# Feed-forward weights loaded, rounded and checked inside the first cross-attention

## The reference, cut to what matters

```python
x = x + tanh(g_xattn[0]) * L0_xattn(layernorm(x), ctx, ctx)      # 16 heads of 16
x = x + tanh(g_ffn[0])   * L0_ffn(layernorm(x))
x = x + tanh(g_xattn[1]) * L1_xattn(layernorm(x), ctx)           # 8 heads of 64
x = x + tanh(g_ffn[1])   * L1_ffn(layernorm(x))                  # gated self-attention
...
# L0_ffn: tlin(x, w, s) = (x @ w.T) * s
h = silu(tlin(x, w1, w1_s)) * tlin(x, w2, w2_s)    # w1, w2: 1024 x 256
h = gelu(tlin(h, h1, h1_s))                        # h1, h2: 1024 x 1024
h = gelu(tlin(h, h2, h2_s))
out = tlin(h, w3, w3_s)                            # w3: 256 x 1024
```

## Time and profile before

| | |
|---|---|
| Time, median of 3 runs | 2078.14 us (2077.79 to 2080.9) |
| Profiled execution, its own time | 2080.15 us |
| Its span in the trace | 2078.3 us |
| Mean granted TensorE clock | 0.956 |
| Busy over the span | PE 1858.6, DVE 1202.1, ACT 1129.6, POOL 736.7 us |

### The profile page before, as it was taken

How to read it: one execution, slowest core, us unless ns; L and a number is a source line. 1 busy time by engine, 2 the same in 40 slices (tenths; PEclk the granted TensorE clock), 3 DMA queues, 4 the chain that set the end, 5 groups by cost and what they waited for, 6 DMA issues and landing times. The chain is left out here.

```text
span 2078.3 us, 61778 instructions
## 1 busy us (share of the span) xinstructions
PE 1858.6 (89%) x27201; PEld 1516.5 (73%) x27201; DVE 1202.1 (58%) x1661; ACT 1129.6 (54%) x1952; POOL 736.7 (35%) x832
## 2 busy tenths in 40 slices
PE   4999509999999999999599986899999999999986
PEld 3677407888878888888477865778888878887865
DVE  4776463423233243332455444888888888887883
ACT  3777444434344344443255542667777777776661
POOL 3777460000100010001233321456655565654541
PEclk9999859999999999999799996999999999999997
DMA  3010240000000000000301003422332242223210
GB/s 88 27 33 23 107 165 1 21 1 21 13 9 20 0 20 20 0 20 0 116 17 38 23 21 102 110 63 64 89 105 59 59 120 79 65 69 99 59 49 23
DMA packets 135939, 104.92 MB, mean 50 GB/s; under 512 B 9379, under 2 KB 132104, under 8 KB 135688
## 3 DMA queue, kind: packets, MB, share of 16 engines
q1 hardware_dynamic: 135688, 101.19, 16.0%
HBM read 76.00 MB, written 25.17 MB: 49 GB/s over the span
## 5 line engine op out<-in xcount | busy, mean ns | idle before, releaser
L1487 ACT ACTIVATE E_prob<-E_ps_s,E_negmax 128x1024 f32<-128x1024 f32 x256 | 284.7, 1115 | 146.9 <-DVE E_negmax L1801 146.5
L1801 DVE TENSOR_REDUCE E_negmax<-E_ps_s 128x1 f32<-128x1024 f32 x256 | 301.4, 1219 | 92.6 <-PE E_ps_s L1306 92.4
L1808 DVE STREAM_TRANSPOSE E_prob<-E_prob 128x1024 f32<-128x1024 f32 x256 | 303.9, 1226 | 23.8 <-ACT E_prob L1487 11.5
L1325 PEld LDWEIGHTS E_ps_o<-E_prob,E_vrep 32*64 32x64 f32 x15872 | 232.1, 130 | 71.5 <-ACT E_part L1513 54.5
L1325 PE MATMUL E_ps_o<-E_prob,E_vrep 32*64 32x128 f32 x15872 | 264.8, 274 | 18.6 <-issue 9.3
L909 ACT ACTIVATE F_raw<-F_ps,ffn_scales 128x512 f32<-128x512 f32 x128 | 88.2, 689 | 288.2 <-PE F_ps L819 288.2
L819 PE MATMUL F_ps<-F_ha,ffn_w_rounded 128*128 128x512 f32 x1024 | 240.5, 396 | 0.0
L819 PE MATMUL F_ps<-F_hb,ffn_w_rounded 128*128 128x512 f32 x1024 | 240.2, 395 | 0.0
L819 PEld LDWEIGHTS F_ps<-F_hb,ffn_w_rounded 128*128 128x128 f32 x1024 | 192.4, 188 | 46.5
L819 PEld LDWEIGHTS F_ps<-F_ha,ffn_w_rounded 128*128 128x128 f32 x1024 | 191.3, 188 | 47.9 <-issue 1.6
L1703 POOL TENSOR_TENSOR E_part<-E_part 128x512 f32<-128x512 f32 x93 | 119.3, 1283 | 255.1 <-ACT E_part L1513 255.1
(11 more groups left out here) (275 smaller groups left out, 3984.6 us busy)
## 6 DMA issues: line engine op xcount, KB each, us to landing
E_vrep<-E_v_all SPq DMA_DIRECT2D x128, 256.0 KB, 3.0
W_stage<-in_L_ffn_h_wT SPq DMA_DIRECT2D x16, 512.0 KB, 6.1
E_v_all<-E_vst SPq DMA_DIRECT2D x32, 256.0 KB, 2.2
F_x<-x SPq DMA_DIRECT2D x9, 512.0 KB, 3.7
A_x<-in_x SPq DMA_DIRECT2D x16, 256.0 KB, 5.4
x<-A_x SPq DMA_DIRECT2D x16, 256.0 KB, 2.2
x<-F_x SPq DMA_DIRECT2D x8, 512.0 KB, 2.9
C_x<-x SPq DMA_DIRECT2D x16, 256.0 KB, 5.4
```

The source lines that it names most:

```text
L1325: mm = pe.matmul(low[64 * j:64 * j + 64, g, :], vrep[rows, slot, KB // 4 * (quarter % 2) + k, dh * j:dh * (j + 1)], prob[rows, u % 2, :, j ...
L1487: act.activation(prob[:, s // UT % 2, s % UT, j, :], ps_s[:, j, :], ACT.Exp, bias=negmax[:, at:at + 1], scale=1.0, accum_out=den[:, 2 * c ...
L1801: dve.tensor_reduce(negmax[:, at:at + 1], ps_s[:, j, :], AX.X, ALU.max, negate=True).then_inc(d_max, 1)
L1808: dve.transpose(at, at).then_inc(d_t, 1)
```

## The change

The block W goes. `cross_attention` takes a further argument `ffn`, given for A alone. In A, SP loads the 22 chunks into a stage of 3 places. At the end of each step T = -4 to 17 ACT rounds one chunk by the same copy as before. DVE no longer takes differences: it ors the 32 bits of the staged chunk into `w_bits` (the first time an and with 0x7FFFFF), at the end of the same step. At the end of T = 18 it masks the 23 mantissa bits of the result and takes the maximum per partition: the flag is zero only if all weights have an empty mantissa. TensorE transposes this column ahead of `scores(28)`, at T = 26, into columns of `ps_s` that no score uses, and DVE takes its maximum into `ffn_inexact`. POOL has no part in it. The flag is then read as before. A place in the stage must be free of both ACT and DVE before a chunk is loaded over it. The buffer of the rounded weights is reserved throughout A.

```diff
+WCH = 1024
+STAGE = 3
+CHECK_FROM = -4
+JUDGED = 28
+MANTISSA = 0x7FFFFF
...
+        if ffn:
+            CHUNKS = len(ffn.src)
+            w_stage = sb("w_stage", [P, STAGE, WCH])
+            w_bits = sb("w_bits", [P, WCH], I32)
+            w_worst = sb("w_worst", [P, 1])
...
+        s_chunk = [sem(f"chunk_in{i}") for i in range(STAGE)]
+        s_scales, a_rounded, d_bits, d_worst, e_worst, d_inexact = (sem(n) for n in (
+            "scales_in", "chunk_rounded", "bits", "worst", "worst_t", "inexact_made"))
...
+            def load_chunk(i):
+                src = ffn.src[i]
+                if i >= STAGE:
+                    sp.wait_ge(a_rounded, i - STAGE + 1)
+                    sp.wait_ge(d_bits, i - STAGE + 1)
+                sp.dma_start(w_stage[:, i % STAGE, :].rearrange("p (k n) -> p k n", n=src.shape[2]),
+                             src).then_inc(s_chunk[i % STAGE], 16)
+
+            def load_scales():
+                for i, v in enumerate(ffn.scale_src):
+                    sp.dma_start(ffn.scales[:, i, :], v).then_inc(s_scales, 16)
+                sp.dma_start(ffn.s3[:, :], spread(ffn.s3_src.rearrange("(a n) -> a n", a=1), 0, P)).then_inc(s_scales, 16)
...
             for n in range(PB, XR):
                 load_x(n)
+            if ffn:
+                for i in range(4 - CHECK_FROM):
+                    load_chunk(i)
             for n in range(NP):
+                if ffn:
+                    for i in range(4 - CHECK_FROM + 2 * n, min(6 - CHECK_FROM + 2 * n, CHUNKS)):
+                        load_chunk(i)
+                    if n == 1:
+                        load_scales()
...
+                if ffn and T == JUDGED:
+                    pe.wait_ge(d_worst, 1)
+                    pe.transpose(ps_s[0:1, 0, 512 - P:512], w_worst[:, :], ident[:, :]).then_inc(e_worst, 1)
...
                 if not odd and 0 <= n + 3 < NP:
                     layer_norm(n + 3)
+                if ffn and 0 <= T - CHECK_FROM < CHUNKS:
+                    i = T - CHECK_FROM
+                    act.wait_ge(s_chunk[i % STAGE], 16 * (i // STAGE + 1))
+                    act.activation(ffn.w[:, i * WCH:(i + 1) * WCH], w_stage[:, i % STAGE, :], ACT.Copy).then_inc(a_rounded, 1)
...
+            def mantissas(i):
+
+                dve.wait_ge(s_chunk[i % STAGE], 16 * (i // STAGE + 1))
+                words = w_stage[:, i % STAGE, :].bitcast(I32)
+                if i == 0:
+                    dve.tensor_scalar(w_bits[:, :], words, MANTISSA, None, ALU.bitwise_and).then_inc(d_bits, 1)
+                else:
+                    dve.wait_ge(d_bits, i)
+                    dve.tensor_tensor(w_bits[:, :], w_bits[:, :], words, ALU.bitwise_or).then_inc(d_bits, 1)
+
+            def mantissa_found():
+
+                dve.wait_ge(d_bits, CHUNKS)
+                own.step(dve.tensor_scalar(w_bits[:, :], w_bits[:, :], MANTISSA, None, ALU.bitwise_and))
+                dve.tensor_reduce(w_worst[:, :], w_bits[:, :], AX.X, ALU.max).then_inc(d_worst, 1)
...
+                if ffn and T + 2 == JUDGED:
+                    dve.wait_ge(e_worst, 1)
+                    dve.tensor_reduce(ffn.inexact[0:1, 0:1], ps_s[0:1, 0, 512 - P:512], AX.X, ALU.max).then_inc(d_inexact, 1)
...
                     residual(n - 2)
-
-
-WCH = 1024
+                if ffn and 0 <= T - CHECK_FROM < CHUNKS:
+                    mantissas(T - CHECK_FROM)
+                if ffn and T == CHECK_FROM + CHUNKS:
+                    mantissa_found()
+            if ffn:
+                dve.wait_ge(d_inexact, 1)
...
-def ffn_weights(nc, fw, w, scales, s3, scale_src, s3_src, inexact, ident, tag):
-
-
-
-
-
-    N = len(fw.src)
-    RING = 4
-    STAGE = 8
...
-        def subtract(eng, i):
-            eng.wait_ge(rounded, i + 1)
-            if i >= RING and on_act(i):
-                eng.wait_ge(sum_of, i // 4)
-            elif i >= RING:
-                eng.wait_ge(max_of, maxima(i - RING))
-            eng.tensor_tensor(rest[:, i % RING, :], stage[:, i % STAGE, :], w[:, i * WCH:(i + 1) * WCH],
-                              ALU.subtract).then_inc(diffed[i % 2], 1)
-
-        @block.sync
-        def _(sp):
-            for i, src in enumerate(fw.src):
-                if i >= STAGE:
-                    sp.wait_ge(diffed[i % 2], (i - STAGE) // 2 + 1)
-                sp.dma_start(stage[:, i % STAGE, :].rearrange("p (k n) -> p k n", n=src.shape[2]),
-                             src).then_inc(loaded[i % STAGE], 16)
-            for i, v in enumerate(scale_src):
-                sp.dma_start(scales[:, i, :], v).then_inc(small, 16)
-            sp.dma_start(s3[:, :], spread(s3_src.rearrange("(a n) -> a n", a=1), 0, P)).then_inc(small, 16)
-            sp.wait_ge(small, 16 * (len(scale_src) + 1))
-
-        @block.scalar
-        def _(act):
-            def row_sum(i):
-                act.wait_ge(diffed[1], i // 2 + 1)
-                act.activation(rest[:, i % RING, :], rest[:, i % RING, :], ACT.Abs,
-                               accum_out=worst[:, i:i + 1]).then_inc(sum_of, 1)
-
-            for i in range(N):
-                act.wait_ge(loaded[i % STAGE], 16 * (i // STAGE + 1))
-                act.activation(w[:, i * WCH:(i + 1) * WCH], stage[:, i % STAGE, :], ACT.Copy).then_inc(rounded, 1)
-                if i >= 2 and on_act(i - 2):
-                    row_sum(i - 2)
-            for i in range(N - 2, N):
-                if on_act(i):
-                    row_sum(i)
-
-        @block.gpsimd
-        def _(pool):
-            for i in range(1, N, 2):
-                subtract(pool, i)
-
-        @block.vector
-        def _(dve):
-            def row_max(i):
-                if not on_act(i):
-                    dve.wait_ge(diffed[i % 2], i // 2 + 1)
-                    dve.tensor_reduce(worst[:, i:i + 1], rest[:, i % RING, :], AX.X, ALU.max,
-                                      apply_absolute_value=True).then_inc(max_of, 1)
-
-            for i in range(N):
-                if i % 2 == 0:
-                    subtract(dve, i)
-                if i:
-                    row_max(i - 1)
-            row_max(N - 1)
-            dve.wait_ge(max_of, maxima(N - 1))
-            dve.wait_ge(sum_of, N // 4)
-            dve.tensor_reduce(worst[:, N:N + 1], worst[:, 0:N], AX.X, ALU.max).then_inc(worst_all, 1)
-            dve.wait_ge(transposed, 1)
-            dve.tensor_reduce(inexact[0:1, 0:1], ps[0:1, 0:P], AX.X, ALU.max).then_inc(worst_all, 1)
-            dve.wait_ge(worst_all, 2)
-
-        @block.tensor
-        def _(pe):
-            pe.wait_ge(worst_all, 1)
-            pe.transpose(ps[0:1, 0:P], worst[:, N:N + 1], ident[:, :]).then_inc(transposed, 1)
...
+            with nc.sbuf_tensor("ffn_w_rounded", [P, fw.cols], F32R) as w:
+                fw.w = w
+                cross_attention(nc, ident, gates[:, 0, 0:1], t["x"], x1, t["ctxT"],
+                                *(t[f"L0_xattn_{n}T"] for n in ("wq", "wk", "wv", "wo")),
+                                tuple(t[f"L0_xattn_{n}"] for n in ("bq", "bk", "bv", "bo")), None, 16, "A",
+                                (gates, t["g_xattn"], t["g_ffn"]), fw)
+                flag = nc.values_load(fw.inexact[0:1, 0:1].bitcast(I32))
+                with nc.If_eq(flag.val, 0):
+                    feed_forward(nc, ident, gates[:, 1, 0:1], x1, x2, fw, w, scales, s3, True, "F")
```

More of the change, by code:

```diff
@@ L2049, in _, with gated_layers @@
             sp.wait_ge(loaded, 16 * len(fw.src))
-def ffn_either_way(nc, ident, gate, x_src, x_dst, t):
-    fw = FfnWeights(*(t[f"L0_ffn_{n}T"] for n in ("w1_w", "w2_w", "h1_w", "h2_w", "w3_w")))
-    scale_src = [t[f"L0_ffn_{n}_s"] for n in ("w1", "w2", "h1", "h2")]
-    with ExitStack() as ctx:
-        scales = ctx.enter_context(nc.sbuf_tensor("ffn_scales", [P, 4, fw.K["h1"]], F32))
-        s3 = ctx.enter_context(nc.sbuf_tensor("ffn_s3", [P, D], F32))
-        inexact = ctx.enter_context(nc.sbuf_tensor("ffn_inexact", [1, 1], F32))
-        with nc.sbuf_tensor("ffn_w_rounded", [P, fw.cols], F32R) as w:
-            ffn_weights(nc, fw, w, scales, s3, scale_src, t["L0_ffn_w3_s"], inexact, ident, "W")
-            flag = nc.values_load(inexact[0:1, 0:1].bitcast(I32))
-            with nc.If_eq(flag.val, 0):
-                feed_forward(nc, ident, gate, x_src, x_dst, fw, w, scales, s3, True, "F")
-        with nc.Else():
-            with nc.sbuf_tensor("ffn_w_full", [P, fw.cols], F32) as w:
-                load_full(nc, fw, w)
-                feed_forward(nc, ident, gate, x_src, x_dst, fw, w, scales, s3, False, "G")
-def gated_layers(nc, t, only=None):
+def gated_layers(nc, t):
     T = t["x"].shape[0]
     x1, x2, x3 = (nc.dram_tensor(f"x{i}", [T, D], F32, kind="Internal").ap() for i in range(1, 4))
+    fw = FfnWeights(*(t[f"L0_ffn_{n}T"] for n in ("w1_w", "w2_w", "h1_w", "h2_w", "w3_w")),
+                    [t[f"L0_ffn_{n}_s"] for n in ("w1", "w2", "h1", "h2")], t["L0_ffn_w3_s"])
     with ExitStack() as ctx:
@@ L2094, in gated_layers @@
-        if only is not None:
```

(20 more changed lines are left out.)

38 lines of the change are left out of this document (6 added, 32 removed).

## The result

| | Before | Changed |
|---|---|---|
| Median of 4 runs | 2077.97 us | 2054.95 us (2052.02 to 2059.8) |
| Ratio of the runs | | 0.989, 95% interval 0.9867 to 0.9912 |
| Span of the profiled execution | 2078.3 us | 2057.9 us |
| Mean granted TensorE clock | 0.956 | 0.963 |

The change makes the kernel faster by 23.0 us, 1.1% (0.9 to 1.3%). The forecast was 26.3 us.

The account below looks back on a forecast made before the run. TensorE was taken to set A's pace, with only weight preparation in W. Removing W saves 45.2 us, A grows by 18.9, so 26.3 us less: 2051.8 us against the median 2078.14; 8 in 10 range 2041 to 2068.

Parts of the forecast that it names:

- W's price: Between A and F: removing block W brings F's first load forward, 45.2 us saved (44.1 to 45.7).
- The loop: A's even-to-odd step chain through TensorE, DVE and ACT grows from 10.9 to 13.9 us and sets the pace; +15.5 us.
- The other or and the other copy of the pair find cover: In A's pairs, they fit DVE's 1.67 us idle after odd `shift` and ACT's idle, mostly in the even step.
- The start: A before T = 0: ors directly ahead of `row_max` cost 1.2 us at T = -1, 0.9 at -3 and -2 together.
- T = 18: A's step with the and and maximum in the or's place, no ACT copy: +1.3 us over an ordinary pair.
- The queue: SP's queue in A: chunk loads are hidden and the stores of x behind them are not held; no cost.
- The clock: Rival: stretches of A drop to 1.2 GHz, about 12.1 us longer per pair, and the kernel gets slower; chance 0.05.
- 1.00 from 72 us on: Sign in A: TensorE's granted clock would be 1.00 from 72 us on.
- if they go beyond 15 (the lock): Sign of being wrong: A's pairs last beyond 15 us, where 13.2 to 14 was forecast while chunks come.
- The lock: Rival: in A, ors and POOL operations wait for each other, A grows by 30 to 39 us; chance 0.17.

Follow-up runs that it names:

- no_or: Changed kernel with DVE's 21 ors left out, loads and ACT's copies kept; 2035.87 us, ratio 0.9821 to the kernel before.
- copy_early: Changed kernel with ACT's odd-step copy moved ahead of `q_evacuate` and even-step copy ahead of `exp`; 2044.52 us, ratio 0.9852 to the kernel before.
- odd_all: Changed kernel with chunks only in odd steps from T = 4, context load first, copies early, tiny operations moved; 2032.00 us, ratio 0.9790 to the kernel before.
- ctx_first: Changed kernel with SP issuing a batch's context load ahead of the two weight chunks of its turn; 2046.92 us, ratio 0.9861 to the kernel before.
- moments: Changed kernel with four small DVE variance operations behind the next `row_max`, operands mostly in PSUM; 2044.13 us, ratio 0.9846 to the kernel before.
- best3: Changed kernel with context load first, copies early and tiny operations moved, chunks still in all steps -4 to 17; 2040.09 us, ratio 0.9832 to the kernel before.
- no_lock: Changed kernel with each of 21 ors replaced by a one-input DVE maximum over the same chunk; 2046.81 us, ratio 0.9868 to the kernel before.

## Why the prediction was right

- *W's price.* 45.2 us was forecast, 45.05 is seen. F's start stayed cold, as said, and the cost of reading the flag was within 0.2 us.
- *The loop.* Right in kind: with an or between `residual` and `row_max` and a copy between `o_evacuate` and `prob_out` the pairs grew, with the ors out (no_or) the pairs lost most of it, and with the copies elsewhere (copy_early) some; with both out of the loop, the context in time and the tiny operations moved (odd_all) they are back. Right nearly in size, by luck in part: the four pairs were to take 56.8 us, and take 58.7 where the context is in time (77.68 to 136.35 in ctx_first). But 2 to 3 us of that are the tiny operations, which the sum didn't have; without them (moments) the first three pairs take 12.92, 13.86 and 13.20 us, 13.3 on the mean, not 13.9. A loop priced too dear made up for a term left out. Three terms were off. The or costs 1.6 us, not 1.97. The loop had a branch through `q_proj` that is 0.65 us longer without the or. And the pairs differ: 12.93 with V, 15.55 with the variances, where the sum had one length for all.
- *"The other or and the other copy of the pair find cover."* Right for DVE: the odd or of 2.2 us is nearly free in odd_all. For the other copy no run takes it apart from the odd one.
- *The start.* 2.1 us and two pairs, 5.5 us by the first `residual`; 2.3 and 3.9 are seen. Too dear.
- *T = 18.* Right: 1.3 us over an ordinary pair was forecast. The pair from the `residual` of T = 18 to the next takes 15.13 us, in both profiles, and 13.73 before (160.05 to 173.78): 1.4, and 1.4 again in no_or (15.12).
- *The queue.* The step that failed: "the stores of x behind them are not held". The stores aren't, but the context load is, 2.6 to 4.1 us of wait at `k_proj(2)`. With the half clock behind it this costs 2.1 to 3.7 us. In listing what stands behind the chunk loads on SP it was left out. Copies waited for no DMA but the first.
- *The clock.* The rival's price was real in single stretches: 0.66 at 60 to 70 us, 0.72 around the late context, 0.74 from 252 to 258 us. It made part of the difference between two profiles of one kernel, 5.7 us, and never came near four pairs. The sign "1.00 from 72 us on" failed: it is 0.97 from 72 to 122 and 0.91 from 122 to 172 us.
- *The signs of being wrong.* One was "if they go beyond 15 (the lock)", and two of the first four pairs did, 15.55 and 19.00. The first is the lock, but on the tiny operations and not on the ors as feared; the second is the late context, where two causes meet that the prediction had not put together, a queue and the clock. That the time came out right doesn't undo this.
- *The lock.* Its case was given 0.17. The or itself stayed under its price; what POOL did to the tiny operations, once they were late, is why the loop came out above 56.8.

A's growth was 26.0 us in one profile and 20.3 in the other, against 18.9; the forecast was 1 to 7 us too little, by the context, the tiny operations and half clock, less what start and loop were priced too dear. The time came out 3.1 us above the forecast.

## What to carry to other kernels

Work moved into the idle time of busy engines is not paid by its length but by its place: the same or cost 0.2 to 1.1 us between `residual` and `row_max` (best3 against odd_all) and 0 to 0.3 us behind the odd `shift` (odd_all against the kernel before), though it lasted 2.2 us there. So lay out the loop that returns to its start through all engines, both branches where two join, and put the new instructions outside it. And for each new DMA on a queue, name every transfer that stands behind it until it can be issued, the rare ones too: one small load, in one of sixteen turns, cost 2 to 4 us here. Look also for short operations that the new work pushes into another engine's way: four operations of 0.17 us cost 2 to 3 us a time here.

## What the runs showed of the hardware

A one-input DVE operation on 8 float32 per partition, SBUF to SBUF, took 1.52 us beside a POOL operation of 1.52 us, and 0.17 without one; an and over 1024 int32 took 1.90 us beside POOL's fold in place of 0.69. One-input maxima of the same 1024 numbers, 21 of them while POOL worked (no_lock), took 1.20 to 1.21 us each. The Trainium skill (SBUF — State Buffer, section SBUF: two separate sides) names both cases, two SBUF inputs or a mode with two ports, as taking the lock that POOL shares; these rows agree, and show that an operation on 8 numbers waits as one on 1024 does. The same kernel, run twice, got its half-clock stretches at different places, and A was 5.7 us longer in one of them.
